# Attention in tiles of 128 queries: ScalarE's last exponential ahead of the spread of the queries

## The chip, the cores and the metric

The kernel runs on 1 core of a Trainium2 chip. The metric is device time in microseconds (us); the median of three runs stands for a kernel.

## The reference

One layer on 2048 tokens of width 256: layer norm with modulation, attention in a sliding window with 16 heads of 16, then layer norm and a mixture of 16 experts with the best 4 for each token, plus a shared one. The change lies in the attention:

```python
x = x + ga * _L0_attn_ref(h, L0_attn_w_qkv, L0_attn_w_out)
...
scores = jnp.einsum('bhncd,bhnkd->bhnck', qc, kc) * SCALE      # chunks of 64 queries, 128 keys
scores = jnp.where(mask[None, None], scores, -jnp.inf)
attn = jax.nn.softmax(scores, axis=-1)
out = jnp.einsum('bhnck,bhnkd->bhncd', attn, vc)
```

## The kernel before, in words

It is written by hand as one program for each engine, with semaphores between them; each engine works through its own in the order of the code. Three stages follow each other: `project_qkv`, `attention_and_routing`, `experts_and_output`. The change is in the program of ScalarE in the second.

That stage has 16 tiles (`each_tile`, n = 0 to 15). A tile is two chunks of 64 queries, one from each half of the sequence, so 128 queries, and 16 heads in four groups q = 0 to 3. What the engines do for it:

- TensorE, `scores(n, t, q)` (L1275 the mask, L1278 four heads): scores with the queries on the partitions, into the banks `SB`. Only their maxima are wanted. They run one to two tiles ahead: `scores(n + 2, ., 0)` and `scores(n + 2, ., 1)` stand at the end of tile n.
- VectorE, `row_max` (L1035): the maxima of these. TensorE turns them (`transpose_max`, L1307), ScalarE copies them to `mT` (`max_out`, L867), and SyncE's queue brings them as one row to the tile `MM` (`put_max`, L738). Two `MM` take turns. One lies in a place that the profile calls `gu_hi`, so the transfer is called `MM<-mT` behind the even tiles and `gu_hi<-mT` behind the odd ones.
- TensorE, `scores_t(n, t, q)` (L1288 mask and maxima out of `MM`, L1290 four heads): the scores again, with the keys on the partitions, into two banks `TB` in turn. `scores_t(n, t, 0)` is the first thing of tile n and waits for the row in `MM`.
- ScalarE, `exps(n, q)` (L907): the exponential of such a bank, 128x512, into `prob`. It signals `exp_done`.
- TensorE, `weigh(n, q)` (L1300): the product of `prob` with the values; it waits for `exps(n, q)`.
- VectorE normalises the result (`normalise`, L1044 and L1048), TensorE turns and projects it (L1312, L114), VectorE adds the residual (L1063). Every second tile the routing of an earlier pair of tiles is worked off between these: on ScalarE `h2_hi`, `router_exp` and `normalise_x1`, on TensorE `router` and `ranks`.

The queries need a form in which the two heads that share 32 rows are kept apart: `spread_queries` (L149) is an activation that multiplies a copy of the queries, 97x1024, by zero or one and writes it to `Q2`, once for each half c = 0, 1. (In the profile its output is `gu_hi` and its input `dn_hi`.) `spread(n + 2, ., 0, .)` and `spread(n + 2, ., 1, .)` in tile n signal `q_spread`. Two wait for that signal:

```python
            if runs(n, 0, TILES - 3):
                eng.wait_ge(q_spread, 2 * n + 6)
...
                scores(n + 2, (t + 2) % 4, 0)
```

on TensorE right behind `weigh(n, 3)` (L1399), and on SyncE `queries_in` (L812), which loads the copy of the next pair of tiles over the old one (L135), in odd tiles, and behind which the stores `keep_x1` and `keep_h2` are queued.

The order on TensorE at the end of a tile is: `scores_t(n, t, 3)`, `weigh(n, 2)`, in odd tiles from 5 on `ranks`, `weigh(n, 3)`, `scores(n + 2, ., 0)`, in odd tiles from 3 on `transpose_h2`, `scores(n + 2, ., 1)`, and then `scores_t(n + 1, ., 0)` of the next tile.

Of the kernel before, what the change touches and what calls it, by code (L numbers as in the profile page):

```python
# [63 lines left out]
def plain(eng):  # L64

    eng.nop(nofuse=True)


def each_tile(body):


    for n in range(TILES):
        body(n, n % 4, n // 2, n // 4)
# [14 lines left out]
def runs(n, low, high=None):  # L88

    return not isinstance(n, int) or (n >= low and (high is None or n <= high))  # L90
# [55 lines left out]
def spread_queries(eng, T, t, c):  # L146


    eng.activation(T["Q2"][t][:, :, c, :], T["QC"][:, :, t % 2, :], ACT.Copy, scale=T["half"][0:VALID + 1, c:c + 1]).then_inc(T["q_spread"], 1)  # L149
# [9 lines left out]
def split_hi(eng, T, e):  # L159

    eng.activation(T["gu_hi"][:, e, :], T["raw"][:, e, 0:W_GU], ACT.Copy).then_inc(T["w_hi2"], 1)
    eng.activation(T["dn_hi"][:, e, :], T["raw"][:, e, W_GU:W_EXP], ACT.Copy).then_inc(T["w_hi2"], 1)
# [20 lines left out]
def load_raw(eng, A, T, low, high, loaded):  # L183

    at = slice(low, high)
    eng.dma_start(T["raw"][:, at, 0:W_GU], A["egu"][:, at].rearrange("p e k x -> p e (k x)")).then_inc(loaded, 16)
    eng.dma_start(T["raw"][:, at, W_GU:W_EXP], A["ed"][:, at].rearrange("p e k x -> p e (k x)")).then_inc(loaded, 16)
# [456 lines left out]
def attention_and_routing(nc, A, T, ctx, own):  # L644
# [91 lines left out]
    def put_row(eng, p2):  # L736

        eng.dma_start(MM[p2][MASKS:MASKS + 1, :].bitcast(F32).rearrange("o (h x) -> o h x", h=HEADS),  # L738
                      mT[:, p2, :].bitcast(F32)).then_inc(mm_ld[p2], 16)
# [122 lines left out]
    def scalar(eng):  # L862
        def max_out(n, e, p2):
            eng.wait_ge(mt_mm, n + 1)
            if runs(n, 2):
                eng.wait_ge(mm_ld[p2], 16 * e)
            eng.activation(mT[:, p2, :], SB[1][0:HEADS, 0:P], ACT.Copy).then_inc(mt_cp, 1)  # L867

        def o_hi(m):
            eng.wait_ge(to_mm, m + 1)  # L870
            eng.activation(oT[:, 0, :, :], Y[:, 0:D].rearrange("p (k x) -> p k x", k=KD), ACT.Copy).then_inc(oT_hi, 1)

        def normalise_x1(p, u):
            eng.wait_ge(ln2_dve, L2_OPS * (p + 1))
            if runs(p, 1):
                eng.wait_ge(ln2_mod, p)
            for a in range(2):
                eng.activation(xn2[:, a, :], x1[:, 2 * u + a, :], ACT.Identity, bias=ln_nm[:, a:a + 1],
                               scale=ln_rs[:, a:a + 1]).then_inc(ln2_act, 1)

        def h2_hi(p):
            eng.wait_ge(th2_mm, p + 1)
            eng.activation(h2T[:, 0], X[:, :].rearrange("p (a k x) -> p a k x", a=2, k=KD), ACT.Copy).then_inc(h2T_hi, 1)

        def router_exp(g, part):

            if part == 0:
                eng.wait_ge(r_mm, g + 1)
                v = X[:, 0:4 * NE].rearrange("p (a u x) -> p a u x", a=2, u=2)
                eng.activation(rt[:, 0, :, :], v[:, :, 0, :], ACT.Exp, scale=-1.0).then_inc(r_act, 1)  # L890
            else:
                eng.wait_ge(r_dve, R_OPS * g + 7)
                eng.activation(rt[:, 6, :, :], rt[:, 5, :, :], ACT.Exp).then_inc(r_act, 1)

        def spread(n, t, c, count):

            if count is not None:
                eng.wait_ge(q_ld, LD * count)
            if runs(n, 4):
                eng.wait_ge(st_mm, 4 * n - 12)  # L900
            spread_queries(eng, T, t, c)

        def exps(n, q):
            eng.wait_ge(st_mm, 4 * n + q + 1)
            if runs(n, 1):
                eng.wait_ge(pv_mm, 4 * n + q - 3)
            eng.activation(prob[:, q, :], TB[q % 2][:, :], ACT.Exp, scale=SCALE).then_inc(exp_done, 1)  # L907

        max_out(0, 0, 0)

        eng.wait_ge(mt_cp, 1)
        eng.wait_ge(mm_set, 2)
        plain(eng)
        put_row(eng, 0)

        for p in range(2):
            eng.wait_ge(qk_st[p], 32 * (GROUPS // 2))

        def tile(n, t, e, i):
            even = t % 2 == 0  # L920
            ahead = runs(n, 0, TILES - 3)
            if even and runs(n, 4):
                h2_hi(e - 2)
            exps(n, 0)
            if ahead and not even:
                spread(n + 2, (t + 2) % 4, 0, e + 1)
            exps(n, 1)
            if runs(n, 1):
                o_hi(n - 1)
            if even and runs(n, 4):  # L930
                router_exp(e - 2, 0)
            if ahead and even:
                spread(n + 2, (t + 2) % 4, 0, e + 1)
            if not even and runs(n, 3):
                normalise_x1(e - 1, (t // 2 + 1) % 2)
            exps(n, 2)
            if runs(n, 0, TILES - 2):
                max_out(n + 1, e + t % 2, (t + 1) % 2)
            if ahead:
                spread(n + 2, (t + 2) % 4, 1, e + 1)  # L940
            exps(n, 3)
            if even and runs(n, 4):
                router_exp(e - 2, 1)

        each_tile(tile)
        h2_hi(PAIRS - 2)
        o_hi(LAST)

        eng.wait_ge(pv_mm, 4 * TILES)
        load_raw(eng, A, T, FIRST, FIRST + 4, T["w_rest"])  # L950
        load_raw(eng, A, T, FIRST + 4, NE - 1, T["w_rest"])
        router_exp(PAIRS - 2, 0)
        normalise_x1(PAIRS - 1, 1)
        router_exp(PAIRS - 2, 1)


        eng.wait_ge(T["w_first"], 32 * FIRST)
        split_hi(eng, T, 0)
        h2_hi(PAIRS - 1)
        split_hi(eng, T, 1)  # L960
        split_hi(eng, T, 2)
        router_exp(PAIRS - 1, 0)
        split_hi(eng, T, 3)
        router_exp(PAIRS - 1, 1)
        for e in range(4, FIRST):
            split_hi(eng, T, e)

        for t in range(4):
            eng.wait_ge(x1_st[t], 32 * (TILES // 4) + 32)
        load_raw(eng, A, T, NE - 1, NE, T["w_last"])  # L970
        eng.wait_ge(T["w_rest"], 64)
        for e in range(FIRST, HI_IN_TAIL):
            split_hi(eng, T, e)
# [1133 lines left out]
```

## Time and profile before

| | |
|---|---|
| median of three runs | 607.01 us (603.23 to 621.51) |
| the profiled execution | 612.32 us |
| its span | 610.4 us |
| TensorE busy | 508.3 us (83%) |
| VectorE busy | 408.7 us (67%) |
| ScalarE busy | 276.7 us (45%) |
| GpSimd busy | 291.0 us (48%) |
| exponentials L907 | 64, 592 ns in the mean |
| spreads L149 | 32, 1139 ns in the mean |

The span is the time from the first to the last instruction of the profiled execution. Busy times are sums over an engine's instructions. In the timeline every row is a group of like instructions: start, duration, engine, line, what it writes and reads, how often, and in brackets how long the engine had been idle and whose signal ended that. PE is TensorE, DVE VectorE, ACT ScalarE, POOL GpSimd, and SPq the queue of SyncE. To find a tile: `scores_t(n, ., 0)` loads its weights (L1288) at 134.00 for n = 2, 186.30 for 6, 198.97 for 7, 211.72 for 8, 225.56 for 9, 237.99 for 10, 251.25 for 11, 265.32 for 12, 277.88 for 13.

### The profile page before, as it was taken

How to read it: one execution, taken by the hardware profiler on the slowest of the kernel's cores; microseconds unless marked ns; L12 is line 12 of the kernel's file. 1: busy time of each engine (PE TensorE's matmuls, PEld its weight loads, DVE VectorE, ACT ScalarE, POOL GpSimd, SP SyncE). 2: the span in 40 equal slices, each digit the busy share in tenths (PEclk: the TensorE clock that was granted, in tenths of full speed). 3: DMA queues.
4: the chain of work that ended last, by engine and by line, in shares of the span. 5: the costliest groups of instructions: out<-in, count | busy, mean ns of one | idle time of the engine just before them, and what ended most of it. 6: DMA issues, size and time to landing. Idle time of an engine off the chain costs nothing.

```text
span 610.4 us, 12812 instructions
## 1 busy us (share of the span) xinstructions
PE 508.3 (83%) x3423; PEld 470.5 (77%) x3424; DVE 408.7 (67%) x1263; ACT 276.7 (45%) x733; POOL 291.0 (48%) x352
## 2 busy tenths in 40 slices
PE   3487876997999989898973158899999899999896
PEld 1287875997998888798962047779989899988895
DVE  5897753234476868767676679987776777784653
ACT  0355451344363444444325645456655566653231
POOL 8556672030114536445376704444444444448893
PEclk9799895588799999989975559999999999999999
DMA  7148899358656548462258434434443344447931
GB/s 233 35 120 240 229 254 307 110 149 263 178 152 187 166 156 230 151 185 68 82 153 318 160 92 120 151 108 131 139 140 118 119 130 140 134 147 272 415 134 53
DMA packets 64649, 101.72 MB, mean 167 GB/s; under 512 B 10144, under 2 KB 48800, under 8 KB 63456
## 3 DMA queue, kind: packets, MB, share of 16 engines
q1 hardware_dynamic: 49600, 56.48, 33.0%
q0 software_dynamic: 10624, 37.43, 17.3%
q10 hardware_dynamic: 4368, 7.14, 3.6%
q8 instruction: 26, 0.43, 0.3%
q14 instruction: 31, 0.25, 0.1%
HBM read 62.15 MB, written 40.17 MB: 168 GB/s over the span
## 4 chain that ended last, share of the span: by engine, by line
PE 52%; DVE 18%; issue 12%; DMA 8%; POOL 4%; ACT 2%; SPq 2%; POOLq 0%; DVEq 0%; ACTq 0%
PE GU L114 13%; PE O L1300 8%; PE TB L1290 4%; PE SB L1278 4%; PE TB L1288 3%; DMA MM<-mT 3%; PE SB L1275 3%; PE HT L1840 3%; PE XT L1830 3%; PE YP L1871 2%; PE YP L114 2%; DVE lo L168 2%; DMA raw<-in_x 2%; PE Y L114 2%; DMA dn_hi<-k_scr 1%
## 5 line engine op out<-in xcount | busy, mean ns | idle before, releaser
L1675 POOL DMA_INDIRECT ys_scr<-h,ids_st x60 | 61.0, 1016 | 76.8 <-DVE h L1736 72.9
L155 POOL DMA_INDIRECT xs_scr<-h,slot_u x64 | 62.6, 978 | 63.2 <-PE TB L1290 34.0
L114 PE MATMUL GU<-gu_hi,xT 128*128 x320 | 85.3, 348 | 1.0 <-DVE lo L168 0.5
L1300 PE MATMUL O<-raw,prob 128*128 128x99 f32 x512 | 75.6, 298 | 8.0 <-ACT prob L907 8.0
L1300 PEld LDWEIGHTS O<-raw,prob 128*128 128x128 f32 x512 | 68.9, 210 | 9.7 <-ACT prob L907 9.6
L907 ACT ACTIVATE prob<-TB 128x512 f32<-128x512 f32 x64 | 37.9, 592 | 82.3 <-PE TB L1290 67.0
L1612 ACT ACTIVATE aT<-HT 128x256 fp32r<-128x256 f32 (+1 forms) x96 | 38.5, 402 | 62.4 <-PE HT L1840 41.8
L1035 DVE TENSOR_REDUCE neg_m<-SB 128x4 f32<-128x512 f32 x64 | 42.5, 687 | 26.0 <-PE SB L1278 25.5
L114 PEld LDWEIGHTS GU<-gu_hi,xT 128*128 128x128 f32 x320 | 52.9, 192 | 2.5 <-issue 2.4
L1605 ACT ACTIVATE g_act<-GU 128x176 f32<-128x176 f32 (+1 forms) x96 | 32.7, 341 | 44.1 <-PE GU L114 40.7
L114 PE MATMUL GU<-lo,xT 128*128 x160 | 52.3, 327 | 0.0
L1726 DVE TENSOR_TENSOR h_act<-GU,g_act 128x176 f32<-128x176 f32 x80 | 27.2, 340 | 31.9 <-ACT g_act L1605 17.0
L1278 PEld LDWEIGHTS SB<-dn_hi,gu_hi 97*128 97x128 f32 x256 | 45.3, 221 | 3.6
L1715 DVE TENSOR_TENSOR aT<-HT,aT 128x256 fp32r<-128x256 f32 (+1 forms) x96 | 42.6, 443 | 6.0 <-ACT aT L1612 4.6
L1830 PE MATMUL XT<-ident,x_st 128*128 128x128 f32 x192 | 37.9, 280 | 10.3 <-DMA x_st<-xs_scr 9.8
L1290 PEld LDWEIGHTS TB<-gu_hi,dn_hi 97*128 97x128 f32 x256 | 42.7, 209 | 3.3
L114 PE MATMUL QB<-gu_hi 128*128 128x256 f32 (+1 forms) x192 | 33.2, 333 | 13.3 <-DVE gu_hi L512 11.8
L1599 ACT ACTIVATE xT<-XT 128x256 fp32r<-128x256 f32 x96 | 36.8, 383 | 14.3 <-PE XT L1830 13.7
L114 PEld LDWEIGHTS QB<-gu_hi 128*128 128x128 f32 x192 | 30.7, 208 | 15.1 <-issue 8.2
L1710 DVE TENSOR_TENSOR xT<-XT,xT 128x256 fp32r<-128x256 f32 x96 | 39.7, 414 | 3.1 <-ACT xT L1599 2.8
L1278 PE MATMUL SB<-dn_hi,gu_hi 97*128 97x128 f32 x256 | 41.1, 289 | 0.0
L1290 PE MATMUL TB<-gu_hi,dn_hi 97*128 97x128 f32 x256 | 38.9, 278 | 0.0
(235 smaller groups left out, 1328.6 us busy)
## 6 DMA issues: line engine op xcount, KB each, us to landing
x_st<-xs_scr SPq DMA_DIRECT2D x80, 144.0 KB
planes<-ys_scr POOLq DMA_DIRECT2D x8, 1024.0 KB, 17.1
dn_hi<-k_scr SPq DMA_DIRECT2D x36, 192.0 KB
k_scr<-k_ev SPq DMA_DIRECT2D x8, 768.0 KB, 6.7
dn_hi<-q_scr SPq DMA_DIRECT2D x21, 256.0 KB
q_scr<-q_ev SPq DMA_DIRECT2D x8, 512.0 KB, 3.3
raw<-in_egu SPq DMA_DIRECT2D x8, 352.0 KB, 4.9
raw<-in_x SPq DMA_DIRECT2D x36, 64.0 KB, 3.7
```

Source lines behind the costliest of these rows:

```text
L114: mm = eng.matmul(out, a, b, start=(i + j == 0), stop=(i == len(pairs) - 1 and j == 2))
L155: eng.indirect_dma_start(T["xs_scr"], bass.IndirectOffsetOnAxis(ap=T["slot_u"][:, par, t % 2, k:k + 1], axis=0), T["h2"][:, row, :], None) ...
L907: eng.activation(prob[:, q, :], TB[q % 2][:, :], ACT.Exp, scale=SCALE).then_inc(exp_done, 1)
L1035: eng.tensor_reduce(neg_m[:, p2, 4 * q:4 * q + 4], SB[q % 2][:, :].rearrange("p (h x) -> p h x", h=4), AX.X, ALU.max, negate=True).then_in ...
L1278: mm = eng.matmul(bank[:, hh * P:(hh + 1) * P], queries(t, 4 * q + hh), keys(par, 4 * q + hh, j), start=False, stop=True, skip_group_check ...
L1290: mm = eng.matmul(bank[:, hh * P:(hh + 1) * P], keys(par, 4 * q + hh, j), queries(t, 4 * q + hh), start=False, stop=True, skip_group_check ...
L1300: mm = eng.matmul(O[:, head // 8, at:at + WIDE * VC], prob[:, q, hh * P:(hh + 1) * P], VW[:, bass.ds(HEADS * n + head, WIDE), :].rearrange ...
L1612: eng.activation(aT[0:rows, p2, 0, 0:k, :], HT[p2][0:rows, 0:k * P].rearrange("p (k x) -> p k x", k=k), ACT.Copy).then_inc(aT_hi, 1)
L1675: eng.indirect_dma_start(ys, bass.IndirectOffsetOnAxis(ap=ids_st[:, r:r + 1].bitcast(U32), axis=0), results(r % 8), None).then_inc(sent[q] ...
L1710: eng.tensor_tensor(xT[:, p2, 1, :, :], XT[p2][:, 0:D].rearrange("p (k x) -> p k x", k=KD), xT[:, p2, 0, :, :].bitcast(F32), ALU.subtract) ...
L1715: eng.tensor_tensor(aT[0:rows, p2, 1, 0:k, :], HT[p2][0:rows, 0:k * P].rearrange("p (k x) -> p k x", k=k), aT[0:rows, p2, 0, 0:k, :].bitca ...
L1830: mm = eng.transpose(XT[t % 2][:, k * P:(k + 1) * P], x_st[:, t, k * P:(k + 1) * P], ident[:, :])
```

## The change

In ScalarE's program of a tile the last exponential, `exps(n, 3)`, is written ahead of the spread of the second half of the queries, `spread(n + 2, ., 1, .)`:

```diff
             exps(n, 2)
             if runs(n, 0, TILES - 2):
                 max_out(n + 1, e + t % 2, (t + 1) % 2)
+
+            exps(n, 3)
             if ahead:
                 spread(n + 2, (t + 2) % 4, 1, e + 1)
-            exps(n, 3)
             if even and runs(n, 4):
                 router_exp(e - 2, 1)
```

`ahead` holds for n = 0 to 13. On ScalarE, in the first tiles of the attention (L907 is the exponential, L867 `max_out`, L149 the spread, L871 and L883 copies for the projection and the routing), where the rows of the two kernels stand so:

```order
-L907 ACTIVATE prob<-TB 128x512 x2
-L149 ACTIVATE gu_hi<-dn_hi,half 97x16x64
-L907 ACTIVATE prob<-TB 128x512
-L871 ACTIVATE oT<-Y 128x256
-L907 ACTIVATE prob<-TB 128x512
-L867 ACTIVATE mT<-SB 16x128
-L149 ACTIVATE gu_hi<-dn_hi,half 97x16x64
-L907 ACTIVATE prob<-TB 128x512 x3
```

```order
+L907 ACTIVATE prob<-TB 128x512
+L149 ACTIVATE gu_hi<-dn_hi,half 97x16x64
+L907 ACTIVATE prob<-TB 128x512
+L871 ACTIVATE oT<-Y 128x256
+L907 ACTIVATE prob<-TB 128x512
+L867 ACTIVATE mT<-SB 16x128
+L907 ACTIVATE prob<-TB 128x512
+L149 ACTIVATE gu_hi<-dn_hi,half 97x16x64
```

This is tile 1 in both. Behind L867 the spread came first and then the exponential (before, the x3 holds it and the first two of the next tile); now the exponential comes first. On ScalarE again, at the end of an odd tile from 3 on, where L883 is the first row of the next, even tile:

```order
 L867 ACTIVATE mT<-SB 16x128
-L149 ACTIVATE gu_hi<-dn_hi,half 97x16x64
-L907 ACTIVATE prob<-TB 128x512
+L907 ACTIVATE prob<-TB 128x512
+L149 ACTIVATE gu_hi<-dn_hi,half 97x16x64
 L883 ACTIVATE h2T<-X 128x512
```

The same two rows have changed places, and what stands around them is as before. No other engine's order differs.

## Rows read from the trace of the kernel before

**Rows 1.** Stretches, 103 to 316 us: busy time (count) by engine, clock, DMA share, GB/s.

```profile
103.00:316.00 213.00, 196.28 (x1383) 184.78 (x1383) 129.92 (x414) 87.77 (x156) 74.66 (x117) 0.89 0.55 160
```

**Rows 2.** Who waited for whom: us in total, times, longest.

```profile
PE O L1300 <- ACT prob L907: 8.0, 12, 1.1
```

**Rows 3.** Timeline of TensorE: groups ahead of which it was idle, tiles 6 to 12.

```profile
196.72 1.13 PE L1300 MATMUL O<-raw,prob 128*128 128x99 f32 x8 [1.07 <-ACT prob L907]
...
207.39 1.13 PE L1300 MATMUL O<-raw,prob 128*128 128x99 f32 x8 [0.71 <-ACT prob L907]
...
209.05 1.14 PE L1300 MATMUL O<-raw,prob 128*128 128x99 f32 x8 [0.16 <-ACT prob L907]
...
222.51 1.13 PE L1300 MATMUL O<-raw,prob 128*128 128x99 f32 x8 [0.53 <-ACT prob L907]
...
225.56 0.50 PE L1288 MATMUL TB<-MM,mask_key 127*128 127x512 f32 x1 [0.56 <-DMA MM<-mT]
...
248.40 1.14 PE L1300 MATMUL O<-raw,prob 128*128 128x99 f32 x8 [1.08 <-ACT prob L907]
...
251.25 0.50 PE L1288 MATMUL TB<-MM,mask_key 127*128 127x512 f32 x1 [0.37 <-DMA MM<-mT]
...
275.64 1.14 PE L1300 MATMUL O<-raw,prob 128*128 128x99 f32 x8 [0.96 <-ACT prob L907]
```

**Rows 4.** Timeline of ScalarE in tiles 2, 6 and 7.

```profile
141.31 0.60 ACT L907 ACTIVATE prob<-TB 128x512 f32<-128x512 f32 x1
...
194.88 0.27 ACT L867 ACTIVATE mT<-SB 16x128 fp32r<-16x128 f32 x1 [1.63 <-PE SB L1307]
195.06 1.13 ACT L149 ACTIVATE gu_hi<-dn_hi,half 97x1024 fp32r<-97x1024 f32 x1
196.10 0.57 ACT L907 ACTIVATE prob<-TB 128x512 f32<-128x512 f32 x1
...
199.92 0.60 ACT L907 ACTIVATE prob<-TB 128x512 f32<-128x512 f32 x1 [3.13 <-PE TB L1290]
200.41 1.14 ACT L149 ACTIVATE gu_hi<-dn_hi,half 97x1024 fp32r<-97x1024 f32 x1
...
206.74 0.60 ACT L907 ACTIVATE prob<-TB 128x512 f32<-128x512 f32 x1 [2.87 <-PE TB L1290]
```

**Rows 5.** Timeline of TensorE at the ends of tiles 2 and 6.

```profile
142.87 0.48 PE L1275 MATMUL SB<-mask_key,mask_qry 126*128 126x512 f32 x1
...
194.56 1.08 PE L1300 MATMUL O<-raw,prob 128*128 128x99 f32 x8
...
197.63 0.48 PE L1275 MATMUL SB<-mask_key,mask_qry 126*128 126x512 f32 x1
...
199.03 0.45 PE L1288 MATMUL TB<-MM,mask_key 127*128 127x512 f32 x1
```

**Rows 6.** The same at the end of tile 12.

```profile
276.55 0.47 PE L1275 MATMUL SB<-mask_key,mask_qry 126*128 126x512 f32 x1
...
277.94 0.45 PE L1288 MATMUL TB<-MM,mask_key 127*128 127x512 f32 x1
```

**Rows 7.** The row of maxima in tiles 6, 8, 12: issue, then us to landing; last, all.

```profile
195.22 0.58 SPq L738 DMA_DIRECT2D MM<-mT  x1
...
MM<-mT SPq DMA_DIRECT2D x1, 8.0 KB, 3.5
...
221.02 0.58 SPq L738 DMA_DIRECT2D MM<-mT  x1
...
MM<-mT SPq DMA_DIRECT2D x1, 8.0 KB, 4.5
...
274.14 0.58 SPq L738 DMA_DIRECT2D MM<-mT  x1
...
MM<-mT SPq DMA_DIRECT2D x1, 8.0 KB, 2.7
...
DMA to landing us min/median/max: 1.9/3.2/7.4
```

## The prediction

> **What bounds the kernel now.** I read the table of stretches first. The attention stage lasts from about 103 to 316 us; in it TensorE is busy for 196.28 of 213.00 us and ScalarE for 87.77 [rows 1]. So ScalarE is no bottleneck by its load, and a change of its order is worth only the time in which TensorE stands still for it. The list of waits gives that time: TensorE idles 8.0 us in 12 places until an exponential (`prob`, L907) is done [rows 2]. The timeline of TensorE shows the 12 one by one [rows 3]. Five of them (the one at 207.39 stands for them; the others are 0.71, 1.03, 1.03 and 0.41) stand ahead of the third group of products with the values, `weigh(n, 2)`, and wait for the third exponential, which the change doesn't touch: 3.89 us. Seven stand ahead of `weigh(n, 3)` and wait for the last exponential: 1.07 in tile 6, 0.16 in tile 7, 0.53 in tile 8, 1.08 in 10, 0.96 in 12, and in tiles 9 and 11 rows like that of tile 7, with 0.15 and 0.16. Their sum is 4.11 us, and together with 3.89 they are the 8.0 of the list. Nothing of that kind stands before tile 6 or behind tile 12.
>
> Why the last exponential is late there is seen on ScalarE [rows 4]. In tile 6 the copy of the maxima starts at 194.88, the spread at 195.06, and the exponential at 196.10; it has waited for nothing but the spread, since its scores were there: TensorE went on from them to `weigh(6, 2)` at 194.56, and was through with that at 194.56 + 1.08 = 195.64 [rows 5]. The spread holds ScalarE for 1.04 us (195.06 to 196.10), a little less than its duration of 1.13, because neighbours overlap.
>
> **The change, term by term.** It adds and removes no instruction. In 14 tiles (0 to 13, those with a spread) two neighbours on ScalarE swap: an exponential of 0.57 to 0.60 us and a spread of 1.13.
>
> 1. The exponential starts up to 1.04 us earlier. In tile 6 it would run from 195.06 to 195.66, and `weigh(6, 3)` could start at once behind `weigh(6, 2)`: 195.68 in place of 196.72. TensorE's 1.07 us go there.
>
> 2. The spread starts later by what an exponential holds the engine, 0.49 us (199.92 to 200.41 in tile 7, the row of an exponential and the spread behind it) [rows 4]. In tile 6: from 195.55 to 196.68. The one who waits for it is TensorE, ahead of `scores(n + 2, 0)`, directly behind `weigh(n, 3)`. `weigh(6, 3)` now has TensorE from 196.72 to 197.63, that is 0.91 [rows 3, 5]; started at 195.68 it would be through at 196.59. The spread is then the later one, by 0.1. With some 0.05 us for the signal, `scores(8, 0)` starts at 196.73 in place of 197.63: 0.90 of the 1.07 are left. In tile 12 the wait is 0.96 [rows 3], and less the same 0.1 I take 0.85. Odd tiles lose nothing to it.
>
> 3. Where the last exponential is not held by the spread, nothing is gained and the spread comes later. This is so in tiles 0 to 5. Tile 2 is the tightest that I worked out: exponential at 141.31 [rows 4], spread from 141.80 to 142.93, and TensorE comes to `scores(4, 0)` at 142.87 [rows 5]: even within 0.1 us. I take zero for it, with bounds of 0 and 0.1 a tile, 0.6 in six tiles.
>
> 4. What follows on TensorE is `scores(n + 2, 0)`, `scores(n + 2, 1)` and then `scores_t(n + 1, 0)`, which needs the row of maxima that SyncE's queue has brought to `MM`. That transfer starts behind the copy of the maxima, and the copy stands ahead of both swapped instructions. So its landing doesn't move, and it caps the gain. Issue and landing [rows 7]: tile 6 at 195.22 + 3.5 = 198.7, and TensorE now starts on it at 199.03 [rows 5], so at most 0.3 are to be had, and with the weight load ahead of it 0.2. Tile 8: 4.5 us from 221.02, and TensorE already waits 0.56 for it at 225.56 [rows 3]: the gain is zero, the 0.53 just become more waiting for the DMA. Tile 10: the same, 0.37 us of waiting now, gain zero. Tile 12: 274.14 + 2.7 = 276.8, TensorE gets there at 277.94 [rows 6], so 1.1 us are free and the 0.85 pass. Odd tiles 7, 9 and 11: TensorE doesn't wait for the row behind them, so 0.16 + 0.15 + 0.16 = 0.47 pass. More is not to be had there, since the four small matmuls of `ranks` fill TensorE ahead of `weigh(n, 3)`.
>
> 5. SyncE issues the next queries behind both spreads of an odd tile (L812). That issue (L135, three pieces) moves later by about half a microsecond, and with it the stores of x1 and h2 queued behind it on SyncE. The queries are needed one tile later, the stores much later, and the next row of maxima leaves SyncE a whole tile later (195.22, then 221.02 for the even tiles 6 and 8 [rows 7]). I take zero; if that cover were gone it would be 0.5 in each of 6 odd tiles, 3 us.
>
> 6. `router_exp(., 1)` in even tiles stands behind both and keeps its place. Zero.
>
> The sum: 0.2 (tile 6) + 0 (8) + 0 (10) + 0.85 (12) + 0.47 (odd tiles) = 1.5 us gained. The profiled execution took 612.32 us with a span of 610.4, so the same execution would be 610.8. The median of the three runs shown is 607.01, 5.3 below it; the same 1.5 us off that is 605.5.
>
> **A rule against a row.** The 8 KB row of maxima lands 1.9 to 7.4 us after its issue, 3.2 in the median, and behind tiles 6, 8 and 12 after 3.5, 4.5 and 2.7 [rows 7]. The Trainium skill (DMA: Bandwidth & Descriptors, Anatomy of one DMA) puts the fixed part of a transfer at about 2.0 us for GpSimd's path, and little for so few bytes. The quickest agrees, the three that matter don't. By that rule the cap of step 4 would be off and the full gain of the first rival below would come.
>
> A second one concerns when scores reach ScalarE. In tile 7 the third exponential starts at 206.74, 2.87 us after ScalarE was free, and the profile puts that down to the matmuls of its scores (L1290), behind which TensorE has two more groups [rows 4]. The Trainium skill (Perfetto Trace Analysis, Tensor Engine Instruction) says that a matmul's end in a profile is an estimate and its signal comes after it; the row agrees as to the sign. I cannot say from the rows what delays them. Tiles 6 to 13 have it, and it ends before the swapped pair starts.
>
> **The rivals.**
> A, the whole wait comes back: the row of maxima lands early enough in tiles 6, 8 and 10 too. Then it is 0.90 + 0.53 + 0.90 + 0.85 + 0.47 = 3.65 us, 603.4. For it: landings vary between 1.9 and 7.4 us [rows 7], and less idle ahead of it changes which traffic it meets. Against: in tiles 8 and 10 TensorE waits for it already.
> B, nothing comes back: the start of each tile is set by the row of maxima or by VectorE, and what TensorE saves it waits for there. 607.0. For it: tiles 8 and 10 do that, and behind tile 12 the chain runs over VectorE's normalisation and maxima.
> C, slower: the spread takes the exponential's place as the late one. Place: TensorE's wait for the spread ahead of `scores(n + 2, 0)`. Its price is from 0 to the whole spread, 1.13 us a tile. It decides from the point at which the last exponential starts more than about 0.1 us later than `weigh(n, 2)`: if the late signals of tiles 6 to 13 reach the last exponential too, ScalarE stands still where it now spreads. At 1.13 in these 8 tiles that is 9.0, less the 1.5: 7.5 slower, 614.5. With 14 tiles it would be 15.8 less 1.5, 14.3 slower: the outer bound. Against it: in all of tiles 6 to 12 the exponential starts within 0.1 us of the spread's end.
> That the change doesn't do what it says is excluded: the order shows the swap in all 14 tiles.
>
> **How the numbers follow.** My forecast of a small gain near 1.5 us 0.55, A 0.15, B 0.2, C 0.1. The predicted time is 605.5. The runs shown lie between 603.23 and 621.51, so the median of some runs can itself be off by several microseconds; the range goes from A less some 2.5 to B and part of C: 601 to 611. A measurement of this kernel can tell about 2% from no change, 12 us; only noise or the outer bound of C gets there: faster 0.02, same 0.95, slower 0.03.
>
> **What would show it.** Right: TensorE's waits for `prob` fall from 8.0 us in 12 places to about 3.9 in 5; ScalarE's exponential follows the copy of the maxima within 0.2 us in tiles 6 to 12; a short wait for the spread (L149), about 0.1, shows ahead of L1275 in tiles 6, 10 and 12; the waits of L1288 for the DMA of `mT`, now 0.56 and 0.37 behind tiles 8 and 10, become about 1.1 and 1.3, and one of some 0.7 appears behind tile 6. Wrong: waits for the spread over 0.5 us each, or an attention stage shorter by over 3 us or longer than before.

## The result, and the profile after

| | before | after |
|---|---|---|
| median of 4 runs, taken in turn | 613.07 us (603.23 to 621.51) | 638.02 us (635.69 to 642.31) |
| the profiled execution, its span | 612.32, 610.4 us | 635.69, 633.8 us |
| TensorE busy | 508.3 us | 528.9 us |
| granted clock, mean | 0.904 | 0.861 |

The changed kernel is slower: 1.0552 times the time before, 95% interval 1.044 to 1.0664. I had forecast 605.5 us, 1.5 less than before, with a range of 601 to 611. The sign and the size are both wrong.

The direct effect came as forecast all the same. This is the list of waits of the changed kernel, 100 to 345 us (one line is added in its code, so every line behind it has a number one higher: L1289, L1291 and L1301 are L1288, L1290 and L1300 of before):

```profile
PE TB L1289 <- DMA MM<-mT: 17.2, 6, 4.9
...
PE O L1301 <- ACT prob L907: 0.6, 1, 0.6
```

TensorE's waits for an exponential fell from 8.0 us in 12 places [rows 2] to 0.6 in one. In their place stands a wait for the row of maxima, `MM<-mT`: 17.2 us in 6 places. The same list of before has 4.6 in 4 for it:

```profile
PE TB L1288 <- DMA MM<-mT: 4.6, 4, 3.3
```

TensorE's timeline of the changed kernel shows where. Each of these rows is the first of an odd tile (3, 5, 7, 9, 11, 13), and stands at the place of 199.03 and 225.56 of before [rows 3, 5]:

```profile
152.32 0.79 PE L1289 MATMUL TB<-MM,mask_key 127*128 127x512 f32 x1 [4.91 <-DMA MM<-mT]
...
181.11 0.51 PE L1289 MATMUL TB<-MM,mask_key 127*128 127x512 f32 x1 [0.87 <-DMA MM<-mT]
...
207.07 0.79 PE L1289 MATMUL TB<-MM,mask_key 127*128 127x512 f32 x1 [3.35 <-DMA MM<-mT]
...
238.39 0.50 PE L1289 MATMUL TB<-MM,mask_key 127*128 127x512 f32 x1 [3.14 <-DMA MM<-mT]
...
268.27 0.50 PE L1289 MATMUL TB<-MM,mask_key 127*128 127x512 f32 x1 [2.52 <-DMA MM<-mT]
...
298.10 0.79 PE L1289 MATMUL TB<-MM,mask_key 127*128 127x512 f32 x1 [2.42 <-DMA MM<-mT]
```

The wait is not all of it. The view of stretches of the changed kernel (columns as in [rows 1]: us, busy time and count of PE, PEld, DVE, ACT, POOL, then the granted clock) shows the tiles 7, 8, 9, 11 and 13:

```profile
207.00:221.00 14.00, 13.93 (x68) 13.37 (x69) 6.39 (x22) 5.71 (x10) 7.71 (x12) 0.57 0.36 110
223.50:238.00 14.50, 11.75 (x96) 11.18 (x94) 10.23 (x33) 5.55 (x11) 3.97 (x4) 1.00 0.65 188
238.00:251.00 13.00, 12.61 (x64) 12.11 (x64) 6.94 (x25) 5.17 (x10) 8.07 (x13) 0.61 0.37 118
268.00:281.00 13.00, 12.73 (x65) 12.27 (x65) 7.88 (x27) 5.58 (x10) 7.77 (x12) 0.61 0.38 119
298.00:311.00 13.00, 12.90 (x55) 12.29 (x56) 7.48 (x26) 4.45 (x8) 8.25 (x14) 0.50 0.14 47
```

Before, tiles 7, 8, 9 and 11 looked like this:

```profile
199.00:211.70 12.70, 11.73 (x91) 10.78 (x90) 10.64 (x41) 6.25 (x11) 7.51 (x11) 1.00 0.52 154
211.70:225.50 13.80, 12.06 (x96) 11.24 (x94) 8.17 (x24) 5.32 (x11) 4.96 (x9) 1.00 0.63 189
225.50:238.00 12.50, 11.25 (x89) 10.67 (x90) 10.76 (x40) 6.13 (x11) 7.55 (x11) 1.00 0.58 168
251.20:265.30 14.10, 12.86 (x89) 12.20 (x89) 11.16 (x40) 6.09 (x11) 8.29 (x14) 0.88 0.61 169
```

Before, tiles 7 and 9 ran 12.5 to 12.7 us at a granted clock of 1.00, the level of 2.4 GHz. Tiles 11 and 13 took 14.1 and 14.4 us, with a mean of 0.88: from 261.2 to 264.6 and from 288.5 to 291.9 TensorE was at the other level, 1.2 GHz, though no gap ahead of that in either tile was over 1.03 us. After, each odd tile from 7 on begins behind a halt of 2.42 to 3.35 us and then runs at 0.50 to 0.61: for most or all of it TensorE is at 1.2 GHz, and a stretch of 13 or 14 us holds 55 to 68 matmuls where 12.5 us held 89. Tile 5, behind a wait of 0.87, has no such fall: its queries leave 8.84 us behind its start, those of tile 7 14.39. The even tiles 4 to 14 stay at 1.00. The sum over the span nearly closes: 12.6 us more waiting for the row (17.2 less 4.6), 7.4 less for exponentials (8.0 less 0.6) and 20.6 more busy time of TensorE (528.9 less 508.3) make 25.8, and the span is 23.4 longer; the 2.4 between them are less of other waits. Nearly all of it lies in the attention: the last L1288 of before starts at 308.3, its counterpart of after at 331.1. Not all of it comes by the row, though: tile 1, which waits for no row in either kernel, takes 16.6 us in place of 13.6, since TensorE reaches 2.4 GHz at 133.7 in place of 128.1. `even_only` below has that too (16.0 us) and loses nothing in the whole, so these 3.0 us aren't shown to come from the queue.

Why the row lands late is read on SyncE's queue. In the changed kernel, the queries' issue (L135) and the row's (L738), tiles 5 to 8:

```profile
189.95 1.27 SPq L135 DMA_DIRECT2D dn_hi<-q_scr  x3
...
199.45 0.58 SPq L738 DMA_DIRECT2D MM<-mT  x1
...
218.13 0.57 SPq L738 DMA_DIRECT2D gu_hi<-mT  x1
221.46 1.27 SPq L135 DMA_DIRECT2D dn_hi<-q_scr  x3
...
230.97 0.58 SPq L738 DMA_DIRECT2D MM<-mT  x1
```

And before, tiles 5 and 7 (the row of tile 6 is at 195.22 [rows 7]):

```profile
181.82 1.27 SPq L135 DMA_DIRECT2D dn_hi<-q_scr  x3
...
207.56 0.57 SPq L738 DMA_DIRECT2D gu_hi<-mT  x1
208.59 1.91 SPq L135 DMA_DIRECT2D dn_hi<-q_scr  x3
```

Before, in tile 7 the queries left 1.03 us behind the row; after, 3.33. What is queued from the queries to the next row, with KB each and the median from issue to landing, is in the profile's list of transfers of the changed kernel, 189.5 to 199.6:

```profile
dn_hi<-q_scr SPq DMA_DIRECT2D x3, 256.0 KB
dn_hi<-k_scr SPq DMA_DIRECT2D x3, 192.0 KB, 4.4
xs_scr<-in_pads SPq DMA_DIRECT2D x1, 288.0 KB
h_scr<-h SPq DMA_DIRECT2D x2, 128.0 KB
x_scr<-raw SPq DMA_DIRECT2D x2, 64.0 KB
x_res<-in_x SPq DMA_DIRECT2D x2, 64.0 KB, 7.0
...
MM<-mT SPq DMA_DIRECT2D x1, 8.0 KB, 7.6
```

That is 2144 KB ahead of 8 KB on one queue. Not all of it is in the row's way when the row is issued. The trace's DMA packets show the row of tile 6 as 16 packets of 512 bytes. In the changed kernel 13 of them start from 200.71 to 200.85, 1.3 us behind the issue, and the last three at 202.34, 205.34 and 206.23; at 207.05 the row has landed. Behind tiles 6, 8, 10 and 12 the last packet starts 4.6 to 5.5 us behind the first, in the kernel before 0.8 to 2.4. Meanwhile most of the core's 16 DMA engines are idle. The view of transfers of the changed kernel, 203 to 207, with packets, MB and the share of the 16 engines:

```profile
q1 hardware_dynamic: 63, 0.19, 12.0%
q0 software_dynamic: 19, 0.06, 3.4%
```

The two shares make 15.4%, two or three engines of 16. The blank rows (`in_pads`, 288 KB) are six packets of 49152 bytes, each 1.8 us or longer and never more than two under way: they run on two engines only, and behind them come the packets of the keys (6144 bytes), in turn with those of GpSimd's queue (4608 bytes). So the queue is cleared early on most engines and late on two, and a row whose packets go over all of them lands with the last. The loosened kernels below have no blank rows there.

Set the landing of the row against the issue of these queries, and a near constant comes out, which it isn't against the row's own issue:

| row of tile | before: from its issue | before: from the queries' | after: from its issue | after: from the queries' |
|---|---|---|---|---|
| 6 | 3.5 | 16.9 | 7.6 | 17.1 |
| 8 | 4.5 | 16.9 | 7.4 | 16.9 |
| 10 | 4.3 | 16.3 | 6.7 | 16.2 |
| 12 | 2.7 | 16.3 | 6.7 | 16.6 |

So the row lands 16.2 to 17.1 us behind the queries, whichever kernel it is. From the queries' issue until TensorE was ready for the row it was 17.2, 16.4, 16.0 and 17.3 us before (for example 225.56 less 0.56 less 208.59 = 16.4), which is little margin or none (0.3 and 1.0 us behind tiles 6 and 12, none behind 8 and 10), and 13.8, 13.8, 13.8 and 14.2 after (207.07 less 3.35 less 189.95 = 13.8). The 2.4 to 3.3 us that are missing are the waits. For tile 8 the 2.6 us less have two parts: the queries leave 2.1 us ahead of the even tile's start in place of 3.2 (1.1), and the even tile itself has TensorE ready for the row after 11.7 us (238.39 less 3.14 less 223.57) in place of 13.2 (1.5). Here the Trainium skill (DMA: Bandwidth & Descriptors, Queues, rings and completion order) has a rule that I had not weighed: on each DMA engine, what was issued on one queue is taken up in ring order. The table agrees with it, and so do the row's late packets: the order holds for each engine by itself.

ScalarE's timeline of the changed kernel, tile 7, shows what delays the queries so much:

```profile
217.79 0.27 ACT L867 ACTIVATE mT<-SB 16x128 fp32r<-16x128 f32 x1 [1.38 <-PE SB L1308]
219.75 0.60 ACT L907 ACTIVATE prob<-TB 128x512 f32<-128x512 f32 x1 [1.69 <-PE TB L1291]
220.25 1.14 ACT L149 ACTIVATE gu_hi<-dn_hi,half 97x1024 fp32r<-97x1024 f32 x1
```

Before, the same tile:

```profile
207.23 0.25 ACT L867 ACTIVATE mT<-SB 16x128 fp32r<-16x128 f32 x1
207.39 1.13 ACT L149 ACTIVATE gu_hi<-dn_hi,half 97x1024 fp32r<-97x1024 f32 x1
208.43 0.57 ACT L907 ACTIVATE prob<-TB 128x512 f32<-128x512 f32 x1
```

Before, the spread used the time in which ScalarE would have waited for the last scores. Now the exponential stands ahead of it and waits 1.69 us for them, the spread ends at 221.39, and the queries leave at 221.46.

Some executions of a kernel run at a lower clock throughout and take some per cent longer; below, medians are over all executions and ratios over the others alone, and the profiled ones of `q_late`, `after_pads`, `early`, `early_light` and `before_l3` were of the slow kind, so from them I read which waits stand where, and no kernel's time.

### The profile page after: what moved, and what is told of

The parts are those of the page before. It is cut to its first block, busy times and chain, and to the rows that moved or that the text cites. A ratio compares the mean times of both kernels' runs of the same rounds, so it can differ in the third digit from the quotient of the medians.

```text
span 633.8 us, 12812 instructions
## 1 busy us (share of the span) xinstructions
PE 528.9 (83%) x3423; PEld 493.1 (78%) x3424; DVE 411.8 (65%) x1263; ACT 279.0 (44%) x733; POOL 293.5 (46%) x352
## 4 chain that ended last, share of the span: by engine, by line
PE 57%; DVE 16%; DMA 12%; issue 6%; POOL 5%; ACT 2%; SPq 1%; POOLq 0%; DVEq 0%; ACTq 0%
PE GU L114 13%; PE O L1301 8%; DMA MM<-mT 7%; PE TB L1291 4%; PE SB L1279 4%; PE TB L1289 3%; PE HT L1841 3%; PE XT L1831 3%; PE SB L1276 3%; PE YP L1872 2%; PE YP L114 2%; PE QB L114 2%; PE Y L114 2%; DVE lo L168 2%; PE X L114 2%
## 5 line engine op out<-in xcount | busy, mean ns | idle before, releaser
L155 POOL DMA_INDIRECT xs_scr<-h,slot_u x64 | 64.1, 1001 | 80.3 <-PE TB L1291 40.5
L1301 PE MATMUL O<-raw,prob 128*128 128x99 f32 x512 | 82.6, 319 | 0.6 <-ACT prob L907 0.6
L907 ACT ACTIVATE prob<-TB 128x512 f32<-128x512 f32 x64 | 38.2, 596 | 101.1 <-PE TB L1291 91.9
L1301 PEld LDWEIGHTS O<-raw,prob 128*128 128x128 f32 x512 | 77.2, 232 | 0.7 <-ACT prob L907 0.7
L1291 PEld LDWEIGHTS TB<-gu_hi,dn_hi 97*128 97x128 f32 x256 | 49.8, 242 | 4.0
L1279 PEld LDWEIGHTS SB<-dn_hi,gu_hi 97*128 97x128 f32 x256 | 47.7, 232 | 3.8
L1291 PE MATMUL TB<-gu_hi,dn_hi 97*128 97x128 f32 x256 | 44.6, 307 | 0.0
L1600 ACT ACTIVATE xT<-XT 128x256 fp32r<-128x256 f32 x96 | 36.8, 384 | 15.4 <-PE XT L1831 15.1
L1279 PE MATMUL SB<-dn_hi,gu_hi 97*128 97x128 f32 x256 | 43.1, 299 | 0.0
L114 PEld LDWEIGHTS QB<-gu_hi 128*128 128x128 f32 x192 | 31.7, 214 | 13.2 <-issue 9.0
```

The source lines that it names most:

```text
L114: mm = eng.matmul(out, a, b, start=(i + j == 0), stop=(i == len(pairs) - 1 and j == 2))
L155: eng.indirect_dma_start(T["xs_scr"], bass.IndirectOffsetOnAxis(ap=T["slot_u"][:, par, t % 2, k:k + 1], axis=0), T["h2"][:, row, :], None) ...
L1279: mm = eng.matmul(bank[:, hh * P:(hh + 1) * P], queries(t, 4 * q + hh), keys(par, 4 * q + hh, j), start=False, stop=True, skip_group_check ...
L1291: mm = eng.matmul(bank[:, hh * P:(hh + 1) * P], keys(par, 4 * q + hh, j), queries(t, 4 * q + hh), start=False, stop=True, skip_group_check ...
L1301: mm = eng.matmul(O[:, head // 8, at:at + WIDE * VC], prob[:, q, hh * P:(hh + 1) * P], VW[:, bass.ds(HEADS * n + head, WIDE), :].rearrange ...
```

## The experiments

Theory 1, the queue and the clock: the swap moves the queries' issue in odd tiles; the row of the next even tile is queued behind it and lands late; TensorE halts for it, runs the odd tile at the lower clock, and the odd tile's slowness delays the next queries again. The rivals stand in the expectations. Each kernel ran in three timed rounds beside the kernel before; that one's median was 612.8 to 617.4 from batch to batch, so that ratios count for more than medians.

### The change in even or in odd tiles alone

The diff is that of `even_only`; `odd_only` has the two conditions exchanged.

```diff
+            if even:
+                exps(n, 3)
             if ahead:
                 spread(n + 2, (t + 2) % 4, 1, e + 1)
-            exps(n, 3)
+            if not even:
+                exps(n, 3)
```

> The change in even tiles alone; in odd tiles the spread stays ahead of the last exponential. Theory 1 (queue): the loss comes from odd tiles, where SyncE issues the next queries behind the spread; in both traces the row of maxima of the next even tile lands 16.2 to 17.1 us after that issue. With the old order in odd tiles the issue stays some 1 us behind the row's own issue, TensorE waits under 1 us a tile for the row, and the time is that of before, 603 to 613 us. Theory 2 (ScalarE's order as such, the same in each tile): half of the loss, 622 to 628. Theory 3 (the clock falls for a reason of its own): no forecast, anything up to 638.

> The change in odd tiles alone. Theory 1: the whole loss, 632 to 642 us; the issue of the queries 2.5 us or more behind the issue of the odd tile's row, the even tile's row 16.2 to 17.1 us after it, TensorE waits 2.4 us or more for it in most even tiles, and the odd tiles behind run at a granted clock near 0.6. Theory 2: half of it, 622 to 628.

Measured: even tiles alone 612.63 us (607.06 to 619.43) beside 612.82, not told apart; odd tiles alone 635.04 (633.21 to 638.93), 1.0354 times (1.027 to 1.0437). The list of waits of the kernel with the change in even tiles:

```profile
PE TB L1292 <- DMA MM<-mT: 5.7, 4, 3.0
```

and with it in odd tiles:

```profile
PE TB L1292 <- DMA MM<-mT: 16.2, 6, 3.9
...
PE O L1304 <- ACT prob L907: 1.0, 2, 0.5
```

The loss comes with the odd tiles, the ones whose spread SyncE's queries wait for. The ratio is less than the changed kernel's 1.0552; that one was not run in this batch, so it isn't shown whether the even tiles add to the loss where the odd ones have brought it about. The gain of the even tiles, which I had put at 1.05 us, is too small for the medians to show. Tile 7 of `even_only` starts behind a wait for the row of 0.98 us, and from 201.0 TensorE is at 1.2 GHz for 10 us:

```profile
201.00:211.00 10.00, 10.00 (x47) 9.68 (x46) 7.22 (x24) 4.83 (x9) 6.85 (x9) 0.50 0.51 152
```

So a slow tile can come of a halt shorter than 2.4 us, too.

### The queries alone issued later

The kernel before, with ScalarE's order untouched; SyncE's issue of the queries waits besides for `weigh(n, 3)` of its odd tile:

```diff
             eng.wait_ge(q_spread, 4 * g)
+            if g >= 2:
+                eng.wait_ge(pv_mm, 8 * g - 8)
```

> The kernel before, ScalarE's order untouched; only SyncE's issue of the next queries waits in addition for the last product with the values of its odd tile (1.7 us later than now in tile 7). Theory 1: most of the loss without any change on ScalarE, 625 to 645 us, with the same waits for the row of maxima and the half clock. Theory 2: no change, 603 to 613.

Measured: 637.29 us (626.83 to 640.31), 1.0287 times (1.0148 to 1.0425). Its waits, and the start of tile 7 on TensorE's timeline:

```profile
PE TB L1290 <- DMA MM<-mT: 17.6, 6, 3.9
```

```profile
212.29 0.51 PE L1290 MATMUL TB<-MM,mask_key 127*128 127x512 f32 x1 [3.91 <-DMA MM<-mT]
```

A later issue of the queries, with nothing else changed, gives the same picture and, by the ratio, about half of the loss. This is the run that shows the cause: neither the spread's lateness for TensorE nor the exponential's place is needed.

### The row on ScalarE's queue

The changed kernel, with `put_row` issued by ScalarE right behind `max_out`, on a queue that carries none of the 2144 KB:

```diff
                 max_out(n + 1, e + t % 2, (t + 1) % 2)
+                eng.wait_ge(mt_cp, n + 2)
+                plain(eng)
+                if n >= 1:
+                    eng.wait_ge(st_mm, 4 * n)
+                put_row(eng, (t + 1) % 2)
...
-            if runs(n, 0, TILES - 2):
-                put_max(n + 1, (t + 1) % 2)
```

> The changed kernel, but the row of maxima goes out on ScalarE's own DMA queue right behind its copy, and no longer on SyncE's. Theory 1, with the row held up by what SyncE's queue has in front of it: it lands within some 2 to 3 us, TensorE doesn't wait for it, no half clock behind tile 3, and the time is at or below that of before, 590 to 610 us. Rival 1b: what holds the row up is the load on the shared DMA engines and not the queue; then it lands 6 to 8 us after its issue as now, and the time stays at 632 to 642.

Measured: 627.47 us (618.93 to 635.04) beside 612.82, about half of the loss gone and not all of it as I had expected (590 to 610), and waits for the row of 7.5 us in place of 17.2. The row's landing, issued by ScalarE (ACTq), median of 8:

```profile
MM<-mT ACTq DMA_DIRECT2D x8, 8.0 KB, 4.9
```

Against 6.7 in the changed kernel, and behind tiles 6 to 12 4.7 to 5.4. It isn't the 2 us of a row that meets no traffic (the odd tiles' `gu_hi<-mT` lands after 1.9). So the order within the queue is part of the delay, and a part is left on another queue too. The same page and section of the Trainium skill says that SyncE and ScalarE have one ring each on the same 16 DMA engines, which take turns between their rings; that would be this rest, and the packets of this run agree. Of the row of tile 8, issued at 227.72, the first packet starts at 228.91 and the last two at 231.56 and 231.81, and on the two engines that have the blank rows and then the keys, packets of SyncE's, GpSimd's and ScalarE's queues alternate there.

### The clock alone

The changed kernel, with TensorE busy ahead of the wait for the row, on 24 matmuls into a bank that is written anew behind them:

```diff
+            if not even and 3 <= n <= 13:
+                for _ in range(24):
+                    eng.matmul(TB[0][:, 0:D]..., tri[:, 0, :], tri[:, :, :], ...)
             eng.wait_ge(mm_ld[p2], 16 * e + 16)
```

> The changed kernel, and in the odd tiles 3 to 13 TensorE runs 24 matmuls of 128x256 (their result is overwritten) ahead of its wait for the row of maxima. It tells how much of the loss is the idle time itself and how much the half clock behind it. Theory 1a (clock): the row lands as late as now and TensorE gets on no earlier, but with the clock up each odd tile runs some 4 us shorter, so the queries are issued earlier and the next row lands earlier: 612 to 622 us. Theory 1b (the clock doesn't matter, the queue is the bound): 634 to 644. The other risk: where the row is already there the filler itself costs some 2.6 us a tile.

Measured: 618.41 us (615.46 to 620.92), 1.006 times before (0.9989 to 1.0131). Its tile 7 in the view of stretches:

```profile
208.00:223.00 15.00, 14.29 (x112) 13.48 (x112) 11.96 (x35) 7.66 (x13) 9.04 (x16) 1.00 0.62 170
```

The 24 matmuls fill the time of the wait and do nothing useful, yet about 20 us come back (638.0 to 618.4, or 1.0552 to 1.006 times before): from tile 5 on the clock stays at 1.00, and 15 us hold 112 matmuls, the 24 among them. Tile 3 still waits 2.24 us and falls to 1.2 GHz. So most of the loss goes with the clock. What the slow matmuls cost themselves and what comes by the later queries of a slow tile, this run doesn't separate.

### Less in the queue, and where the loss goes then

Three kernels. The first is the changed kernel with the blank rows (`in_pads`) stored behind the even tiles 4 to 10, two pieces of 288 KB in each:

```diff
-            if isinstance(n, int) and 4 <= n < 4 + NE // 2:
+            if n >= 4 and n % 2 == 0:
+                for k in ({4: (0, 1), 6: (2, 3), 8: (4, 5), 10: (6, 7)}.get(n, ())):
```

> The changed kernel, with SyncE's 288 KB stores of pads moved from the odd tiles 5, 7, 9, 11 (ahead of the even tiles' row of maxima in the queue) to the even tiles 4, 6, 8, 10, behind the row. Theory 1 (the row lands when the queue in front of it is empty, 16.2 to 17.1 us behind the issue of the queries, with some 2.1 MB in between): 288 KB less is one part in 7, so it lands 2 to 2.5 us earlier relative to the issue of the queries (14 to 15 us), behind tiles 6, 8, 10 and 12; TensorE's waits there fall from 2.4 to 3.4 us to about 1, the half clock mostly goes, 615 to 630. If the 16.9 us are set by something else (latency of the chain, TensorE's own work), no change: 633 to 642.

Measured: 661.52 us (654.58 to 670.5), 1.0666 times, a miss. The waits for the row behind tiles 6 to 12 are gone: the row lands 1.9 us after its issue. That doesn't price the blank rows, since the row is issued late too, 19.3 to 22.5 us behind the queries. TensorE's timeline says why, with this ahead of `transpose_h2`, and the like at 267.54 (5.00) and 305.37 (5.24):

```profile
230.27 1.09 PE L1325 MATMUL X<-ident,h 128*128 128x128 f32 x4 [5.01 <-POOL h L752]
```

and the list of waits says what GpSimd's new `h2` waited for:

```profile
POOL h L752 <- DMA xs_scr<-h,slot_u: 22.1, 4, 7.5
```

The scatter of the dispatched rows must have left an `h2` tile before it is written anew, two pairs of tiles later. In the changed kernel this wait is 6.3 us, 2.4 at the longest. That the two pieces of 288 KB, now issued together in an even tile, make the scatter land later is what I take from it; no run separates it. The halt has only changed its place. This was the second coupling that I hadn't seen.

The other two try an order that issues the queries earlier: the exponential first in even tiles, and in odd tiles the spread ahead even of the third exponential (`early`), and the same with a lighter queue (`early_light`: blank rows and raw copies of weights moved to even tiles and to tiles 12 to 15).

```diff
+            if ahead and not even:
+                spread(n + 2, (t + 2) % 4, 1, e + 1)
             exps(n, 2)
             if runs(n, 0, TILES - 2):
                 max_out(n + 1, e + t % 2, (t + 1) % 2)
-            if ahead:
+            exps(n, 3)
+            if ahead and even:
                 spread(n + 2, (t + 2) % 4, 1, e + 1)
-            exps(n, 3)
```

> The last exponential ahead of the spread in even tiles, as in the change; in odd tiles the spread of the second half is put further ahead, before the third exponential. Theory 1: the issue of the queries then follows the odd tile's row by about 0.65 us, earlier than in the kernel before (1.0), so the rows land in time and no wait for them is above 1 us behind tile 3: 600 to 612, at or a little under before. Theory 2 (any spread ahead of an exponential costs TensorE): 612 to 620, with waits of L1300's products for the third exponential.

> The same, and SyncE's loads of expert weights (two experts in each of tiles 0 to 3) now in tiles 0, 2, 12, 14, and the pads of the odd tiles 5, 7, 9, 11 in 10 to 15, so that less stands in the queue ahead of an even tile's row. Theory 1: the row of tile 2 lands some 3 us after its issue in place of 7.4, the wait of 3.3 us behind it and the half clock of tile 3 go (4 to 7 us), the other waits go: 592 to 604.

Measured: 620.63 us (606.47 to 627.15) and 626.45 (611.63 to 627.09) beside 615.39, neither told apart from before, where I had expected 600 to 612 and 592 to 604. In the second, `MM<-mT` lands after 1.9 us in the median and the waits for the row are gone from tile 3 on, but `transpose_h2` waits instead, 7.8 us in 4 places.

### Both couplings loosened

The lighter queue, and the `h2` tiles in rotation over three pairs, so that GpSimd waits for the scatter of three pairs ago, put into the kernel before, the changed kernel and `early`:

```diff
-        return slice(4, 6) if p == PAIRS - 1 else slice(2 * (p % 2), 2 * (p % 2) + 2)
+        return slice(2 * (p % 3), 2 * (p % 3) + 2)
...
-        if sent is not None:
-            eng.wait_ge(h2_st[p % 2], 32 * sent + 32)
+        if p >= 3:
+            u, sent = (p - 3) % 2, (p - 3) // 2 + 1
+            eng.wait_ge(h2_st[u], 32 * sent + 32)
...
-            if isinstance(n, int) and n < 4:
-                for x in range(FIRST // 4 * n, FIRST // 4 * (n + 1)):
+            if n in (0, 2, 12, 14):
+                for x in {0: (0, 1), 2: (2, 3), 12: (4, 5), 14: (6, 7)}[n]:
...
-            if isinstance(n, int) and 4 <= n < 4 + NE // 2:
-                two = slice(2 * (n - 4), 2 * (n - 4) + 2)
+            if n in (4, 6, 8, 10, 12, 13, 14, 15):
+                k = (4, 6, 8, 10, 12, 13, 14, 15).index(n)
+                two = slice(2 * k, 2 * k + 2)
```

> The kernel before with a lighter queue on SyncE in the odd tiles (the raw copies and the blank rows go in even tiles or in tiles 12 to 15) and with the h2 tiles in rotation over three pairs, so that GpSimd's new h2 waits for the scatter of three pairs ago. Theory 1 (the queue and the clock): the row of maxima behind even tiles lands in 2 to 3.5 us, TensorE's waits for it stay under 1 us in all, and no wait of transpose_h2 for h2 is over 1 us; 598 to 608 us. Rival (the lightening itself costs something, since the blank rows and the copies meet other traffic): above 612, with waits of TensorE for a DMA or for h2 in the list.

> The same two loosenings in the changed kernel. Theory 1: the swap costs 23 us only because the issue of the next queries, behind the last spread of an odd tile, moves the landing of the row behind the following even tile; with less in the queue in between, the row lands in under 4 us in the even tiles, the waits of TensorE for it fall from 17.2 us to under 4, those for prob stay under 1, and the kernel takes at most 1% more than the same loosening of the kernel before: 598 to 610 us. Rival (the swap costs something of its own that neither the queue nor the h2 tiles explain, such as the later release of the query tiles): still 3% or more above the loosened kernel before, with odd tiles at half clock though the row has landed.

> The same two loosenings, with the exponential ahead of the spread in even tiles, and in odd tiles the spread ahead even of the third exponential, so that the queries are issued earlier than in the kernel before. Theory 1: queries issued some 2 us earlier in odd tiles than in the loosened kernel before, no wait for the row over 0.5 us; 595 to 606 us, and it ties with or beats the loosened kernel before by up to 1%. Rival: the spread ahead of the third exponential makes weigh(n, 2) or the last exponential late in odd tiles (waits for prob of 1 us each in 6 tiles), then 6 to 8 us above the loosened kernel before.

Measured, beside 617.41 us for the kernel before in the same batch:

| | median (lowest to highest) | ratio to before |
|---|---|---|
| before, loosened | 608.39 (604.12 to 616.56) | 0.9852 (0.9783 to 0.9922) |
| changed, loosened | 602.89 (597.88 to 606.75) | 0.9791 (0.9697 to 0.9886) |
| early, loosened | 603.63 (600.08 to 604.70) | 0.9788 (0.972 to 0.9856) |

The profile of the changed, loosened kernel has this for tiles 7 and 8:

```profile
186.00:200.30 14.30, 13.47 (x92) 12.35 (x91) 11.68 (x40) 6.45 (x11) 8.71 (x15) 0.88 0.55 159
200.30:212.50 12.20, 11.56 (x95) 11.07 (x95) 7.18 (x21) 5.08 (x10) 3.96 (x4) 1.00 0.60 166
```

The 0.88 of tile 7 comes of a stretch at 1.2 GHz from 196.7 to 200.1, behind gaps of 0.55 and 0.23 us; no wait for the row stands there. In its list of waits from 125 to 300 us stands:

```profile
PE O L1301 <- ACT prob L907: 4.0, 7, 0.8
...
PE TB L1289 <- DMA MM<-mT: 0.3, 1, 0.3
```

The row lands 1.9 us after its issue in the median of 8, and TensorE's waits for it are down to 0.3 us in all. Against the issue of the queries the rows of tiles 6 to 12 land after 13.3 to 15.5 us (233.96 plus 1.9 less 222.44 for tile 10), where it was 16.2 to 17.1: without the blank rows between them the queue is through earlier. And the same swap that cost 5.5% now costs nothing: 0.9791 against 0.9852 would be 0.6% faster than the loosened kernel before, but the intervals overlap, so it is no difference that these runs show. All three are under the kernel before, the first just above the 598 to 608 that I had expected. The changed, loosened one is the best in the median that was run, and it beats both kernels of the case, though not the other two loosened ones.

### The rotation alone

The changed kernel with the first two edits of that diff alone, the queue as heavy as it was:

> The changed kernel with only the rotation of the h2 tiles over three pairs; SyncE's queue is as heavy as in the changed kernel. Theory 1 (the loss comes in through the queue ahead of the row of maxima): the row still lands 6 to 8 us after its issue behind tiles 6 to 12, TensorE's waits for it stay at 13 to 18 us, odd tiles at half clock, 628 to 640 us. Rival (the gain of the doubly loosened kernel comes from the h2 tiles alone, and the queue is only what the trace names): waits for the row under 6 us and below 612 us.

Measured: 637.15 us (633.29 to 642.41), 1.0551 times (1.044 to 1.0662), which is the changed kernel's own ratio, and:

```profile
PE TB L1290 <- DMA MM<-mT: 16.9, 6, 5.0
```

So the rotation alone takes nothing of the loss away, and the lighter queue is needed for it; with the lighter queue the rotation is there so that the halt doesn't move to `h2`. The lighter queue alone in the changed kernel was not run; `after_pads` and `early_light` are the nearest to it.

## Why the prediction was wrong

The step that failed is step 5, the price of SyncE's later issue of the queries, taken as zero with 3 us as its outer bound; step 4 fell with it. Of steps 1 and 2 the outcome held, the working only in part. ScalarE's timeline of the changed kernel in tile 6:

```profile
199.11 0.27 ACT L867 ACTIVATE mT<-SB 16x128 fp32r<-16x128 f32 x1 [0.43 <-PE SB L1308]
200.46 0.60 ACT L907 ACTIVATE prob<-TB 128x512 f32<-128x512 f32 x1 [1.07 <-PE TB L1291]
200.95 1.14 ACT L149 ACTIVATE gu_hi<-dn_hi,half 97x1024 fp32r<-97x1024 f32 x1
```

The exponential does not follow the copy within 0.2 us, it waits 1.07 for its scores. It still comes in time: both groups of products run from 200.25 without a gap, the spread ends at 202.09, and `scores(8, 0)` begins at 202.14. So the waits for `prob` fell to 0.6 us, further than to the 3.9 that I had left, and rival C's place is empty, though its condition (an exponential over 0.1 us behind `weigh(n, 2)`: here 0.21) was there.

Step 5 failed: "I take zero; if that cover were gone it would be 0.5 in each of 6 odd tiles, 3 us." I had looked for who needs the queries themselves, and they do have a tile's time. What needs the queue is the row of maxima one tile later, and I excused it with "leaves SyncE a whole tile later". A whole tile later isn't behind: the row lands 16.2 to 17.1 us after the queries' issue in both kernels. Both sizes of the step were off as well. The issue moves by 2.3 us against the row ahead of it (1.03 to 3.33 in tile 7), not 0.5, since the exponential ahead of the spread waits 1.69 us for its scores. I had taken 0.49, the time for which an exponential holds ScalarE; that is the whole delay only if its scores are ready when its turn comes. And 3 us was no outer bound, since it priced no clock.

Step 4 failed with it: "So its landing doesn't move, and it caps the gain." I took the landing from the row's own issue (3.5, 4.5, 2.7), a spread of almost 2 us that should have made me ask what sets it. Set against the queries' issue the spread is 0.6. The margins that I did read, 0.3 us in tile 6 and waits of 0.56 and 0.37 behind tiles 8 and 10, said that the kernel stood at the edge there; any delay of the row is paid nearly in full there.

What was missing as well is the price of a halt at that place. The waits alone are 12.6 us more, less the 7.4 that the exponentials gave back; 20.6 us more of busy TensorE came on top, and `after_warm` gives back about 20 us by keeping TensorE busy. The chain then feeds itself: at the lower clock an odd tile's queries leave 13.2 to 14.4 us behind the tile's start (tiles 7, 9 and 11), against 9.3 to 9.6 before.

A row was misread too: the late scores were put down for tiles 6 to 13, but the third exponential of tile 6 (192.66) starts 0.3 us behind the shown end of its scores. Nothing in the sum rests on it.

The rivals: A had 0.15; whether its gain comes once the row is out of the way isn't shown, since the two loosened kernels are not told apart. C had the right sign, but its place (TensorE's wait for the spread) and its outer price, 14.3 us, are both refuted. The chance of 0.03 for slower was too small, because the one way to lose that I priced was TensorE's own wait for the spread. The spread has a second waiter, SyncE, and of that one I priced only the transfer it issues.

## What to carry to other kernels

When a moved step releases a DMA issue, list all that is queued behind that issue until the next transfer that an engine waits for, and take the latter's landing from the first issue, not from its own. Look also at how many DMA engines each of them runs on: here 288 KB on two engines held up a row of 8 KB that had all but three of its packets under way within 1.4 us of its issue. If the time from the first issue to the landing is constant from tile to tile while the transfer's own latency isn't, the queue sets it. And where the engine that would wait is TensorE at the full clock with a margin near zero, price a halt at more than its length: here 12.6 us more of halts went with 20.6 us more of busy TensorE, and in `even_only` a halt of 0.98 us was followed by 10 us at 1.2 GHz.

## What the runs showed of the hardware

- An 8 KB transfer lands 1.9 us after its issue in odd tiles, where the last transfer ahead of it left 5.5 us earlier (212.60 and 218.13 in tile 7), 6.7 to 7.6 with 2144 KB ahead of it on the same queue, and 4.7 to 5.4 from another engine's queue.
- The blank rows go as packets of 49152 bytes, at least 1.8 us each and at most two at a time, where the row's 512-byte packets take 0.03 us and 13 or 14 of the 16 of tile 6 start within 0.15 us.
- In the changed kernel halts of TensorE of 3.35, 3.14, 2.52 and 2.42 us were followed by stretches of 13 to 14 us at a granted clock of 0.50 to 0.61, and one of 0.87 was not; with 24 matmuls without use in their place the clock stayed at 1.00 from tile 5 on. The length of a halt alone doesn't tell it: 0.98 us in `even_only` was followed by 10 us at 0.50, and gaps of 1.03 and 0.16 us in tile 11 of the kernel before by a stretch at 0.50 from 261.2 to 264.6.
- In the kernel before, the third exponentials of tiles 7, 8 and 9 wait 2.87, 2.20 and 2.87 us for scores of matmuls that the profile shows as done; for tile 7 that is the row at 206.74 in [rows 4]. In the changed kernel they start 0.04 us behind the shown end of their scores in tiles 3 to 14, and TensorE is ready for the next row 11.7 us behind the start of tile 8 in place of 13.2. That isn't the swap: it is 11.5 us in `odd_only` too, where ScalarE's order in even tiles is that of before, and the loosened changed kernel, which has the swap, has the late scores again (2.7 us in tile 7). What delays the signal was not found, and no run tried it.
